# Feature attention in an eight-layer kernel: units pair by pair of feature groups, tile 0's maxima turned in two parts, the first pass four units ahead at first

## The chip, the cores and the metric

The kernel runs on one core of one Trainium2 chip. The metric is the device time of one execution, in microseconds (us), as the median of the runs. A core has TensorE (PE; its weight loads are listed as PEld), VectorE (DVE), ScalarE (ACT), GpSimd (POOL) and the queues that start DMAs (SP among them). TensorE's clock is granted in two levels, 0.50 of full speed (1.2 GHz) and 1.00 (2.4 GHz).

## The reference

Eight layers work one after the other on x, 1024 tokens of 256 features (16 sequences of 64), each adding to it. The layer of interest is the seventh, an attention between features, not tokens. Its query is the normalised x, key and value are both the context. Per sequence, the 64 tokens are cut into 8 heads of 8 tokens each:

```python
# q, k, v: (16, 64, 256) = (b, d, m or n); h = 8 heads, so d // h = c // h = 8
qh = q.reshape(b * h, d // h, m)
kh = k.reshape(b * h, d // h, -1)
vh = v.reshape(b * h, c // h, -1)
scale = 1.0 / jnp.sqrt(jnp.asarray(d // h, dtype=q.dtype))
qk = jnp.einsum('bdm,bdn->bmn', qh, kh) * scale      # 256 x 256 for each head
sm = jax.nn.softmax(qk, axis=-1)
ret = jnp.einsum('bmn,bcn->bcm', sm, vh)
```

## The kernel before

All eight layers are one program, with one queue of instructions for each engine and semaphores between them; the order in each queue is written out by hand. `feature_attention` follows a mixture of experts, whose last sums (`combine`) it runs itself through `x_of(t)` on VectorE, and is followed by `peer_mlp`, whose first work it starts at its end.

The 1024 tokens are 8 tiles of 128 (`NT`). A tile holds 16 heads of 8 tokens, that is 16 groups. In a strip of 32 partitions (`R`, four strips r = 0 to 3) there are four groups j = 0 to 3 (`J`), which come in two pairs `jp`. A tile is worked in `UNITS` = 4 units, one for each half of the 256 features (called b or nb) and pair `jp`; `halves(u)` says which unit does which. All matrices are float32, and each such matmul is two records in the trace.

A tile is passed twice.

First pass: `scores(u, r)` (line 2383) is one 32-row matmul for each strip r, four to a unit, one *step* each, `step = 4 * u + r`. It writes one bank of PSUM with 512 columns. `top(u, r)` (line 2238) on VectorE takes the negative maximum of each query's row into `nm`. When a tile's 16 maxima columns are made, `turn_maxima(t)` transposes them on TensorE (line 2417, two 128x128 transposes), ScalarE copies them (`maxima`, line 2312) and spreads them into `tm` (`placed(t, jp)`, line 2319, two copies for each pair), and GpSimd adds them to the masked queries `xm` (`less`, line 2183, once for each pair).

Second pass: `turned(u, pair)` (line 2408) computes the scores the other way round with the maximum already taken away, two strips for pair B (r = 2, 3) and two for pair A (r = 0, 1). `exps(u, ...)` (line 2329) on ScalarE takes the exponential of two banks at once, `values(u, j)` (line 2429) multiplies by the context into bank 7 (`VB`), eight 32-column matmuls a unit. At a tile's end `sums` (line 2336) copies that bank, `sort` (line 2447) picks sums and results apart by a table, `sorted_out` (line 2342) copies them and VectorE divides (line 2245 and on) and adds to `k.X`.

The first pass runs ahead of the second. Before the second begins, `FRONT` = 5 units of the first are issued; in unit 0 of the second loop it issues units 5 and 6, and from then on unit u + 6 (`AHEAD`). In the queue of TensorE, within unit u: two scores, turned(u, B), values(u-1, 0), turned(u, A), the other scores, values(u-1, 1). From unit `LAST` = 26 no scores are left.

Eight banks: the first 16 steps (`WIDE`) go round seven banks, 4, 5, 6, 0, 1, 2, 3. From then on scores have three banks, 4, 5 and 6 (`step_bank`), and the others belong to the second pass. A score waits until `top` has read what its bank held (`last_in_bank`). All on TensorE's queue behind a waiting score waits too.

GpSimd's queue at the start: zeroing `nm` (line 2198), `keys(0)`, two reciprocal roots for the normalisation (line 274), `queries(0)`, `keys(1)`, `queries(1)` (lines 2168 and 2175), memsets (2208, 2209), `values` copies of tiles 0 and 1 (2194), then `less(0)`. On VectorE, `norm(t)` (line 285) writes the normalised tile and `ln_stats_dve` (lines 266 to 268) makes its statistics; `x_of` is lines 1117 and 1118.

## Time and profile before

| | |
|---|---|
| median of 3 runs | 1093.72 us (1091.63 to 1097.1) |
| the profiled execution | 1091.79 us |
| its span (first to last instruction) | 1090.1 us |
| TensorE busy | 989.0 us, 91% |
| VectorE, ScalarE, GpSimd busy | 559.1, 361.1, 265.2 us |
| mean granted clock of TensorE | 0.947 |
| the feature attention's share | from 790.7 us to 948.3 us of the span |

Times in the rows are counted from the span's start. A matmul is listed from its start to its modelled end, so neighbouring ones overlap. A group in a timeline joins like instructions: its length is from the first start to the last end, and xN is their number.

### The profile page before, as it was taken

The page shows a single profiled execution, that of the slowest core. Times are in us where ns is not written, and L with a number is a line of the kernel's source. Part 1 is how long each engine was busy: PE and PEld are TensorE (multiplying, and loading weights), DVE is VectorE, ACT ScalarE, POOL GpSimd, SP SyncE. Part 2 cuts the span into 40 slices and gives each one's busy share as a digit, 9 for nine tenths or more (in the row PEclk, how much of TensorE's full clock was granted, in tenths as well). Part 3 has the DMA queues.
Part 4 walks back from the last instruction along what each step waited for, and adds up shares of the span by engine and source line. Part 5 has one row for each costly group of instructions (what it writes and reads, how often), then busy time and mean ns, then how long its engine had stood idle before and what let it go on. Part 6 is the DMA issues. An engine that isn't in the chain of part 4 may idle for free.

```text
span 1090.1 us, 18558 instructions
## 1 busy us (share of the span) xinstructions
PE 989.0 (91%) x7228; PEld 694.9 (64%) x7228; DVE 559.1 (51%) x1277; ACT 361.1 (33%) x687; POOL 265.2 (24%) x337
## 2 busy tenths in 40 slices
PE   5888999989999999968883999999689999997989
PEld 4665599546766667657663999999533343443467
DVE  7766523455435344465375121212277877666891
ACT  4662133242222121214210211111015666744750
POOL 6421342420000000022531122221252534202440
PEclk9996999999999999989985999999859999998989
DMA  9103033221001010054012866667214000010000
GB/s 281 46 2 107 11 97 93 83 59 31 25 29 40 26 40 11 6 154 145 1 64 83 299 213 227 222 217 271 64 34 154 10 2 1 15 64 1 0 11 29
DMA packets 39997, 88.96 MB, mean 82 GB/s; under 512 B 4712, under 2 KB 27592, under 8 KB 36584
## 3 DMA queue, kind: packets, MB, share of 16 engines
q1 hardware_dynamic: 32520, 73.60, 19.8%
q0 software_dynamic: 4080, 11.15, 3.6%
q10 hardware_dynamic: 3312, 3.02, 0.8%
q8 instruction: 60, 0.98, 0.4%
q14 instruction: 25, 0.20, 0.1%
HBM read 76.35 MB, written 11.40 MB: 81 GB/s over the span
## 4 chain that ended last, share of the span: by engine, by line
PE 75%; DVE 13%; ACT 5%; issue 3%; DMA 2%; POOL 2%; DVEq 0%; ACTq 0%; POOLq 0%
PE bank L358 21%; PE bank L1317 11%; PE bank L1336 7%; PE bank L1661 6%; PE bank L2383 5%; PE bank L2408 3%; PE bank L2429 3%; PE bank L2878 3%; PE bank L1307 3%; PE bank L1672 2%; PE bank L1637 2%; PE bank L2447 1%; PE bank L2884 1%; ACT big L587 1%; DVE big L2238 1%
## 5 line engine op out<-in xcount | busy, mean ns | idle before, releaser
L358 PE MATMUL bank<-XNT,big 128*128 128x512 f32 x296 | 136.8, 611 | 7.1 <-DVE big L2618 5.6
L1317 PE MATMUL bank<-big 128*128 128x128 f32 x1012 | 118.5, 277 | 0.1
L1317 PEld LDWEIGHTS bank<-big 128*128 128x128 f32 x1012 | 116.5, 194 | 0.5 <-issue 0.4
L274 POOL TENSOR_TENSOR rstd<-ve,half 128x1 f32<-128x1 f32 x48 | 27.8, 583 | 300.4 <-DVE ve L268 300.2
L2383 PE MATMUL bank<-big,xs 32*128 32x512 f32 x256 | 88.9, 732 | 12.1 <-DVE xs L285 10.4
L358 PEld LDWEIGHTS bank<-XNT,big 128*128 128x128 f32 x296 | 55.1, 193 | 69.7 <-issue 58.8
L2238 DVE TENSOR_REDUCE big<-bank 128x2 f32<-128x512 f32 x128 | 81.9, 685 | 20.3 <-PE bank L2383 19.6
L1095 DVE TENSOR_TENSOR big<-big,bank 128x640 f32<-128x640 f32 x23 | 18.9, 822 | 136.6 <-ACT big L1205 136.6
L1336 PE MATMUL bank<-big 128*128 (+1 forms) x368 | 87.2, 380 | 1.1 <-DVE big L1102 0.7
L2329 ACT ACTIVATE big<-bank 128x1024 f32<-128x1024 f32 x64 | 64.9, 1024 | 39.2 <-PE bank L2408 38.9
L1336 PEld LDWEIGHTS bank<-big 128*128 128x128 f32 (+1 forms) x368 | 66.3, 190 | 9.0 <-issue 1.9
L2408 PE MATMUL bank<-big 32*128 32x512 f32 x256 | 68.4, 659 | 1.6 <-POOL big L2183 1.4
L358 PE MATMUL bank<-CTXT,big 128*128 128x512 f32 (+1 forms) x192 | 66.9, 492 | 0.0
L1661 PE MATMUL bank<-big 128*128 128x256 f32 x256 | 63.7, 394 | 1.5 <-issue 1.2
L358 PE MATMUL bank<-big,CTXT 128*128 128x256 f32 (+1 forms) x224 | 57.9, 409 | 0.0
L1520 DVE COPY big<-bank 128x512 f32<-128x512 f32 x16 | 11.1, 692 | 88.7 <-PE bank L1646 88.7
L1661 PEld LDWEIGHTS bank<-big 128*128 128x128 f32 x256 | 47.1, 194 | 13.4 <-DVE X L1514 5.4
L1568 ACT COPY big<-bank 128x1024 f32<-128x1024 f32 x16 | 16.2, 1012 | 119.0 <-PE bank L1672 119.0
L977 POOL DMA_INDIRECT yg<-big x23 | 22.7, 986 | 135.3 <-DVE big L1102 127.9
L2383 PEld LDWEIGHTS bank<-big,xs 32*128 32x128 f32 x256 | 31.8, 207 | 35.1 <-issue 19.1
L358 PEld LDWEIGHTS bank<-big,CTXT 128*128 128x128 f32 x224 | 42.5, 190 | 17.3 <-issue 12.9
L358 PEld LDWEIGHTS bank<-CTXT,big 128*128 128x128 f32 x192 | 32.9, 196 | 30.2 <-issue 30.1
(356 smaller groups left out, 1753.0 us busy)
## 6 DMA issues: line engine op xcount, KB each, us to landing
big<-m_gu SPq DMA_DIRECT2D x23, 1408.0 KB, 6.0
big<-m_d SPq DMA_DIRECT2D x8, 768.0 KB
big<-a_qk SPq DMA_DIRECT2D x16, 256.0 KB, 2.9
yg<-big ACTq DMA_DIRECT2D x23, 128.0 KB, 2.0
big<-m_gu SPq DMA_DIRECT2D x8, 352.0 KB
big<-a_o SPq DMA_DIRECT2D x16, 128.0 KB, 2.0
xn<-XNT SPq DMA_DIRECT2D x8, 256.0 KB, 2.1
big<-f_keys SPq DMA_DIRECT2D x1, 2048.0 KB, 10.9
```

Source lines behind the costliest of these rows:

```text
L274: e.tensor_tensor(k.rstd[at % NT][:, :], k.ve[at % NT][:, :], k.half[:, 0:1], ALU.pow).then_inc(k.ln_rstd, 1)
L358: ins = e.matmul(out, a, b, start=start and n == 0, stop=stop and n == len(pairs) - 1)
L1307: ins = e.matmul(bank[:, GU[s % 2], c * F:(c + 1) * F], xgT[s % 2][:, kb, :], WB[:, bass.ds(at[s] + (kb * 2 * F + c * F), F)], start=kb == ...
L1317: ins = e.matmul(gu[:, n if n <= WHOLE else n + 1], gu_slot[s % SLOTS][:, c:c + P], xgT[s % 2][:, kb, :], start=kb == 0, stop=kb == KB - 1)
L1336: ins = e.matmul(bank[:, Y[s % 2], 0:D], hT[s % 2][0:row, b, :], WB[0:row, bass.ds(at[s] + (WGU + b * D), D) if LAG else bass.ds(at[s] * S ...
L1661: ins = e.matmul(bank[:, QK0 + j % 2, q * D:(q + 1) * D], cT[:, t * P:(t + 1) * P], wo[h % 2], start=True, stop=True)
L2238: e.tensor_reduce(nm[t % 2][:, b, c:c + 2 * G:G], k.bank[:, step_bank(step), :].rearrange("p (j n) -> p j n", j=2), AX.X, ALU.max, negate= ...
L2329: e.activation(pt[u % 2][:, r].rearrange("p r j n -> p r (j n)"), k.bank[:, b:b + 2, :], ACT.Exp, scale=float(G) ** -0.5).then_inc(S["ex"], 1)
L2383: e.matmul(bank[:, step_bank(step), :], k.xs[t % 2][q, b * P:(b + 1) * P], cm[t % 2][q, 2 * jp:2 * jp + 2].rearrange("p j n -> p (j n)"), ...
L2408: ins = e.matmul(bank[:, pair_banks(u, pair) + r % 2, :], cr[q, t, jp, nb * P:(nb + 1) * P], xm[t % 2][q, 2 * jp:2 * jp + 2].rearrange("p ...
L2429: ins = e.matmul(bank[r * R:(r + 1) * R, VB, jp * D:(jp + 1) * D], cv[t % 2][:, nb, r * J + 2 * jp + j], pt[u % 2][:, r, j], start=nb == 0 ...
L2878: e.matmul(bank[:, OUT + u % 2, 0:D], hT[:, u // UB, b, c], dn[:, b], start=b == 0, stop=False)
```

## The change

Four things are altered in `feature_attention`, all in the order of work; the matmuls, exponentials and sums stay the same in number and shape.

- `halves(u)` gives the units another order: both feature halves of the first pair, then both of the second. `turned` waits for the second pair's `less` at unit 2 of a tile, not at unit 1.
- The maxima of tile 0 are turned in two parts. The first pair's eight go to a new buffer `nm_first` and are transposed behind the scores of unit 2 (into bank 2), the whole tile's again for the second pair behind turned(0, A) (into bank 7). For tile 0, `maxima` and the transposes are therefore made twice, with two maxima sets; `placed(0, 1)` moves behind the exponentials of unit 0. `turns_made` counts the additional turn in all later waits. GpSimd zeroes one buffer more.
- The first 8 steps go round seven banks, not the first 16.
- Before the second pass, 4 units of scores are issued, not 5; then unit 4 in unit 0, units 5 and 6 in unit 1, 7 and 8 in unit 2, and u + 6 from unit 3 on. VectorE's `top`s follow. `norm(1)` comes after unit 1's maxima, not unit 0's; `x_of(3)` and those after it come one unit later.

```diff
@@ -2086,21 +2086,25 @@
     GT = P // G
     UNITS = 4
     NU = UNITS * NT
-    AHEAD, FRONT = UNITS + 2, UNITS + 1
+    AHEAD = UNITS + 2
     LAST = NU - AHEAD
     STEPS = 4
-    WIDE = STEPS * UNITS
+    WIDE = STEPS * 2
     TB, SBK, SBN, VB = 0, 4, 3, 7
     NTB, OB = TB + 2, TB + 3
     A_, B_ = 0, 1
     at0, done0 = 8 * l, LOADED + 8 * l
-    masks0 = k.count_masks(10)
+    masks0 = k.count_masks(11)
     A, B = Arena(k.big[:, 3384:16200], 16200 - 3384), Arena(k.late, 8800)
     cr, sel = A.take(NT, 2, D), A.take(4, P)
     tm = [A.take(J, D) for _ in (0, 1)]
     xm = [B.take(J, D) for _ in (0, 1)]
     cm = [B.take(J, D) for _ in (0, 1)]
     nm = [A.take(2, P) for _ in (0, 1)]
+    nm_first = A.take(2, P)
+
+    def maxima_of(t, jp):
+        return nm_first if t == 0 and jp == 0 else nm[t % 2]
     nT = [A.take(D) for _ in (0, 1)]
     cv = [A.take(KB, GT, R) for _ in (0, 1)]
     pt = [B.take(RG, 2, D) for _ in (0, 1)]
@@ -2124,7 +2128,7 @@
         e.wait_ge(S[name], start[name] + n)
 
     def halves(u):
-        return u // UNITS, u % UNITS // 2, u % 2
+        return u // UNITS, u % 2, u % UNITS // 2
 
     def step_bank(step):
 
@@ -2135,7 +2139,7 @@
 
     def units_ahead(u):
 
-        return [n for n in ((FRONT, AHEAD) if u == 0 else (u + AHEAD,)) if n < NU]
+        return [n for n in {0: (4,), 1: (5, 6), 2: (7, 8)}.get(u, (u + AHEAD,)) if n < NU]
 
     def pair_banks(u, pair):
 
@@ -2143,8 +2147,12 @@
             return TB + strips(pair)[0]
         return (4, 2, 0)[(2 * (u - LAST) + (pair == A_)) % 3]
 
-    def maxima_bank(t):
-        return spare_bank(UNITS * t - 2, NTB)
+    def maxima_bank(t, part=1):
+        return VB if t == 0 and part == 1 else spare_bank(UNITS * t - 2, NTB)
+
+    def turns_made(t):
+
+        return t + 2
 
     def result_bank(t):
         return spare_bank(UNITS * (t + 1) + 1, OB)
@@ -2194,8 +2202,8 @@
                     ins = e.tensor_copy(places(t % 2)[:, kb * G:(kb + 1) * G, j, 2 * G * j:2 * G * j + G], src[:, :, j])
             ins.then_inc(S["cv"], 1)
 
-        for p in (0, 1):
-            e.memset(nm[p], 0.0).then_inc(k.masks, 1)
+        for n in (nm_first, *nm):
+            e.memset(n, 0.0).then_inc(k.masks, 1)
         after(e, "ld", 16)
         keys(0)
         ln_rstd_pool(e, k, at0, 0)
@@ -2232,10 +2240,10 @@
             t, b, jp = halves(u)
             step = STEPS * u + r
             if t >= 2 and u % UNITS == 0 and r == 0:
-                after(e, "nt_ps", t - 1)
+                after(e, "nt_ps", turns_made(t - 2))
             after(e, "s_ps", step + 1)
             c = r * R + 2 * G * (1 - jp)
-            e.tensor_reduce(nm[t % 2][:, b, c:c + 2 * G:G],
+            e.tensor_reduce(maxima_of(t, jp)[:, b, c:c + 2 * G:G],
                             k.bank[:, step_bank(step), :].rearrange("p (j n) -> p j n", j=2), AX.X, ALU.max,
                             negate=True).then_inc(S["mx"], 1)
 
@@ -2254,8 +2262,8 @@
         def rest(u, half):
 
             t, n = divmod(u, UNITS)
-            if half == 1 and u < UNITS:
-                x_of(u + 4)
+            if half == 1 and u <= UNITS:
+                x_of(u + 3)
             if n == 0 and half == 0 and t + 2 < NT:
                 ln_stats_dve(e, k, ch, t + 2, t % 2)
             if n == 1 and half == 0 and t + 2 < NT:
@@ -2275,19 +2283,18 @@
                 k.front[6]["combine"](t)
                 e.wait_ge(k.x_tile, done0 - NT + t + 1)
 
-        e.wait_ge(k.masks, masks0 + 2)
+        e.wait_ge(k.masks, masks0 + 3)
         x_of(0)
         ln_stats_dve(e, k, ch, 0, 0)
         x_of(1)
         norm(0)
         ln_stats_dve(e, k, ch, 1, 1)
-        for u in range(FRONT):
+        for u in range(UNITS):
             for r in range(RG):
                 top(u, r)
-            if u == 0:
+            if u == 1:
                 norm(1)
         x_of(2)
-        x_of(3)
         for u in range(NU):
             ahead = [(n, r) for n in units_ahead(u) for r in range(RG)]
             for half in (0, 1):
@@ -2305,14 +2312,14 @@
     def act(e):
         e.sem_inc(k.xt_sb, NT)
 
-        def maxima(t):
-            after(e, "nt_ps", t + 1)
+        def maxima(t, part=1):
+            after(e, "nt_ps", turns_made(t) if part else 1)
             if t > 0:
                 after(e, "tm", 2 * t)
-            e.copy(nT[t % 2], k.bank[:, maxima_bank(t), 0:D]).then_inc(S["nm"], 1)
+            e.copy(nT[t % 2], k.bank[:, maxima_bank(t, part), 0:D]).then_inc(S["nm"], 1)
 
         def placed(t, jp):
-            after(e, "nm", t + 1)
+            after(e, "nm", turns_made(t) if t > 0 or jp else 1)
             if t >= 2:
                 after(e, "less", 2 * (t - 2) + jp + 1)
             for j in (2 * jp, 2 * jp + 1):
@@ -2341,16 +2348,19 @@
                 after(e, "v_sb", t)
             e.copy(od, k.bank[:, result_bank(t), :]).then_inc(S["od"], 1)
 
-        maxima(0)
+        maxima(0, 0)
         placed(0, 0)
-        placed(0, 1)
         for u in range(NU):
             t = u // UNITS
             more = t + 1 < NT
             exps(u, ((0, B_),))
+            if u == 0:
+                maxima(0)
             if u % UNITS == 2 and more:
                 maxima(t + 1)
             exps(u, ((1, A_),))
+            if u == 0:
+                placed(0, 1)
             if u % UNITS == 2 and more:
                 placed(t + 1, 0)
             if u % UNITS == 3 and more:
@@ -2388,11 +2398,11 @@
             t, nb, jp = halves(u)
             if u % UNITS == 0 and pair == B_:
                 after(e, "less", 2 * t + 1)
-            if u % UNITS == 1 and pair == B_:
+            if u % UNITS == 2 and pair == B_:
                 after(e, "less", 2 * t + 2)
             if u < LAST:
                 if u % UNITS == 3 and pair == B_ and t + 1 < NT:
-                    after(e, "nm", t + 2)
+                    after(e, "nm", turns_made(t + 1))
                 if u % UNITS == 2 and t > 0 and pair == B_:
                     after(e, "od", t)
                 if u > 0:
@@ -2409,12 +2419,12 @@
                                xm[t % 2][q, 2 * jp:2 * jp + 2].rearrange("p j n -> p (j n)"), start=True, stop=True)
             ins.then_inc(S["t_ps"], 1)
 
-        def turn_maxima(t):
-            after(e, "mx", STEPS * UNITS * (t + 1))
+        def turn_maxima(t, part=1):
+            after(e, "mx", STEPS * (UNITS * t + (UNITS if part else 2)))
             if 0 < t < NT - 1:
                 after(e, "ex", 2 * UNITS * t - 3)
             for b in (0, 1):
-                ins = e.transpose(bank[:, maxima_bank(t), b * P:(b + 1) * P], nm[t % 2][:, b, :], k.ident[:, :])
+                ins = e.transpose(bank[:, maxima_bank(t, part), b * P:(b + 1) * P], maxima_of(t, part)[:, b, :], k.ident[:, :])
             ins.then_inc(S["nt_ps"], 1)
 
         def values(u, j):
@@ -2441,7 +2451,7 @@
             elif t == NT - 1:
                 after(e, "od", t)
             else:
-                after(e, "nm", NT)
+                after(e, "nm", turns_made(NT - 1))
             for part in (0, 1):
                 for jp in (0, 1):
                     ins = e.matmul(bank[:, result_bank(t), part * D:(part + 1) * D], sel[:, 2 * part + jp],
@@ -2450,11 +2460,11 @@
 
         e.sem_inc(k.xt_ps, NT)
         after(e, "ld", 16)
-        for u in range(FRONT):
+        for u in range(UNITS):
             for r in range(RG):
                 scores(u, r)
-            if u == UNITS - 1:
-                turn_maxima(0)
+            if u == 2:
+                turn_maxima(0, 0)
         for u in range(NU):
             t = u // UNITS
             ahead = [(n, r) for n in units_ahead(u) for r in range(RG)]
@@ -2464,6 +2474,8 @@
             if 0 < u < LAST:
                 values(u - 1, 0)
             turned(u, A_)
+            if u == 0:
+                turn_maxima(0)
             for n, r in ahead[2 * (u > 0):]:
                 scores(n, r)
             if u % UNITS == 2 and t + 1 < NT:
```

## Rows read from the trace of the kernel before

**Rows 1.** The page: busy time, share of the span, instructions of each engine.
```profile
PE 989.0 (91%) x7228; PEld 694.9 (64%) x7228; DVE 559.1 (51%) x1277; ACT 361.1 (33%) x687; POOL 265.2 (24%) x337
```
**Rows 2.** Busy time of each engine by stretches; then granted clock, DMA share, GB/s.
```profile
790.67:794.00 3.33, 3.33 (x15) 1.75 (x16) 1.82 (x6) 0.00 (x0) 2.49 (x3) 0.50 0.27 82
794.00:797.60 3.60, 3.44 (x14) 1.46 (x10) 3.60 (x7) 0.00 (x0) 3.37 (x2) 0.97 0.01 2
797.60:801.10 3.50, 3.44 (x9) 1.49 (x6) 3.50 (x7) 0.00 (x0) 3.30 (x17) 0.50 0.00 0
...
806.60:812.30 5.70, 4.92 (x17) 1.88 (x17) 4.59 (x9) 2.55 (x3) 3.07 (x2) 0.50 0.13 27
812.30:818.00 5.70, 5.70 (x11) 2.97 (x12) 4.39 (x9) 0.08 (x1) 0.56 (x1) 0.50 0.21 65
818.00:821.40 3.40, 3.40 (x21) 1.08 (x18) 2.62 (x5) 0.99 (x1) 0.00 (x0) 0.51 0.00 0
...
827.58:924.00 96.42, 96.42 (x779) 38.10 (x779) 75.94 (x134) 62.91 (x86) 42.57 (x52) 1.00 0.12 47
924.00:948.30 24.30, 22.59 (x211) 11.30 (x208) 14.22 (x38) 18.36 (x29) 6.18 (x9) 1.00 0.01 1
```
**Rows 3.** The chain of waits: start us, us, what; unit 3 of the second loop.
```profile
827.58 0.63 PE bank L2383 x2
```
**Rows 4.** Timeline, first scores: start, us, engine, line, instructions joined.
```profile
790.67 2.09 PE L2383 MATMUL bank<-big,xs 32*128 32x512 f32 x8 [10.44 <-DVE xs L285]
...
792.51 2.88 PE L2383 MATMUL bank<-big,xs 32*128 32x512 f32 x11
...
792.75 2.48 DVE L2238 TENSOR_REDUCE big<-bank 128x2 f32<-128x512 f32 x4 [1.33 <-PE bank L2383]
...
795.84 7.26 DVE L2238 TENSOR_REDUCE big<-bank 128x2 f32<-128x512 f32 x12
796.00 1.89 POOL L2175 TENSOR_TENSOR big<-xs,strip 128x1024 f32<-128x1024 f32 x1 [0.23 <-DVE xs L285]
...
799.43 1.46 POOL L2194 COPY big<-CTXT 128x64 f32<-128x64 f32 x8
```
**Rows 5.** Timeline, from the turn of tile 0's maxima to the second pass.
```profile
803.15 0.69 PE L2417 MATMUL bank<-ident,big 128*128 128x128 f32 x2 [2.12 <-DVE big L2238]
...
803.77 2.08 PE L2383 MATMUL bank<-big,xs 32*128 32x512 f32 x6
803.88 0.37 ACT L2312 COPY big<-bank 128x256 f32<-128x256 f32 x1 [28.79 <-PE bank L2417]
804.28 1.70 ACT L2319 ACTIVATE big<-big,strip 128x256 f32<-128x256 f32 x4
805.33 2.49 POOL L2183 TENSOR_TENSOR big<-big 128x512 f32<-128x512 f32 x2 [4.44 <-ACT big L2319]
...
806.65 1.24 PE L2408 MATMUL bank<-big 32*128 32x512 f32 x3
...
810.44 1.94 ACT L2329 ACTIVATE big<-bank 128x1024 f32<-128x1024 f32 x2 [3.15 <-PE bank L2408]
```
**Rows 6.** ScalarE's exponentials by line: duration ns min/median/max, first and last start.
```profile
L2329 ACT ACT_TABLE_LOAD  x1: 1283/1283/1283, 806.0 to 806.0; - x1
```
**Rows 7.** Timeline, unit 1 of the second pass, with the clock back.
```profile
820.31 1.08 PE L2429 MATMUL bank<-big 128*32 128x256 f32 x8
...
821.33 0.70 PE L2383 MATMUL bank<-big,xs 32*128 32x512 f32 x2
...
821.86 0.59 PE L2383 MATMUL bank<-big,xs 32*128 32x512 f32 x2
```
**Rows 8.** Timeline near the stage's end, unit 29.
```profile
933.58 1.28 POOL L2183 TENSOR_TENSOR big<-big 128x512 f32<-128x512 f32 x1 [1.28 <-ACT big L2319]
934.91 1.14 PE L2408 MATMUL bank<-big 32*128 32x512 f32 x8 [0.41 <-POOL big L2183]
935.35 0.59 ACT L2336 COPY big<-bank 128x512 f32<-128x512 f32 x1
```

## Prediction

> **What bounds the kernel now.** I read the page first. TensorE is busy for 91% of the span and the other engines for far less [rows 1], so the question is where TensorE works without a wait and where it doesn't. The clock line of the page is near full almost everywhere, but a slice of it is 27 us long, so I then cut the feature attention into stretches [rows 2]. It runs from 790.67, its first score matmul, to 948.3. Three stretches differ.
>
> From 827.58 to 924 TensorE is busy all the time at a granted clock of 1.00, 96.42 of 96.42 us, with VectorE at 75.94 and ScalarE at 62.91. No wait ends late here; TensorE's own instructions set the length. Reordering the four units of a tile doesn't change their number or shape, so this stretch keeps its length.
>
> From 790.67 to 827.58, which is in the chain of waits the start of unit 3 in the second loop [rows 3], 36.91 us pass. TensorE's granted clock is 0.50 (1.2 GHz) up to 794, 0.97 (all but 2.4 GHz) to 797.6, and 0.50 again until 821.4. This is the first pass, which fills the pipeline, and it is where the change works. It is bound by turns: VectorE needs 0.605 us for each maximum (12 in 7.26 us) [rows 4], and once the first seven banks are used TensorE may write a bank only after the maximum of its last content. After 806.6 three banks rotate. In the stretch 812.3 to 818, TensorE is shown busy throughout, but only 11 records fall in it; it writes one score at a time, in turn with VectorE [rows 2].
>
> From 924 to 948.3 the stage runs dry: 22.59 of 24.30 us busy. One wait there belongs to the change, at 934.91 [rows 8].
>
> **The prices.** At the low clock a score needs 2.08 us from its start until VectorE can read it, whether one, three or four of different row strips run together: three take 2.08, four 2.09 [rows 4, 5]. The next matmul on the same strip starts 1.84 us after it (790.67, then 792.51). At the high clock the same two records take 0.70 and 0.59 and overlap to 1.12 us [rows 7]. I add 0.05 us for each semaphore, from the gap between the end of the transposes, 803.84, and the copy at 803.88 [rows 5]. A bank comes round at the low clock in 0.69 + 0.05 + 2.08 + 0.05 = 2.87 us, for three banks 0.96 us a step. At the high clock that is 1.91, or 0.64 a step. VectorE alone would want 0.605. So a step that rides in a group of four is cheap, and a step that has its bank alone is dear at the low clock.
>
> **The change, part by part.**
>
> *Seven banks for 8 steps, not for 16 (WIDE).* Steps 0 to 7 are as before; the maximum of step 7 ends at 792.75 + 7 x 0.605 + 0.69 = 797.67, since norm(1) no longer stands between. Steps 7 and 8 both fall on bank 4. Step 7 may start at 793.5, when the maximum of step 0 is made, and is through by 795.6 even at the low clock. From there to 797.7 TensorE stands still, where before it kept on, and VectorE waits for step 8 until 799.8. Steps 8, 9 and 10 run together; step 11 follows the maximum of 8 at 800.55.
>
> *Turning the maxima in two parts.* turn_maxima(0, 0) stands behind step 11. Step 11's second half streams until about 802.4, so the two transposes run 802.5 to 803.2, against 803.15 before, and all that follows keeps its length: from the transposes' start to the end of less(0, 0) before it was 806.60 minus 803.15, 3.45 us; two of four placed copies on ScalarE stand ahead of it either way [rows 5]. So less(0, 0) ends at 805.95 and turned(0) starts at 806.03, against 806.65. The half-set of maxima comes 8 steps earlier, but the starvation of banks eats nearly all of it: the gain is 0.6 us. GpSimd isn't in the way. queries(1) follows norm(1) at 798.1 and takes 1.89, the memsets 1.54, the copies 1.46 [rows 4]; it is free at 803.0, and needed at 804.7. The added memset costs at most what the eight of its kind take together, 1.54 us (from 797.89, where queries(1) ends, to 799.43) [rows 4]; it lies ahead of the stage's first score, which waits for TensorE's operands from VectorE, not GpSimd (its releaser is line 285), so I count nothing; uncovered it would be those 1.54 us at most.
>
> *One step fewer ahead (four units, not five; then 4, 5 and 6, 7 and 8).* Steps 12 and 13 start 0.62 after the transposes, at 803.12; 14 behind the maximum of 11 (802.66 + 0.69 + 0.05), at 803.41; 15 behind that of 12 (805.23 + 0.74), at 805.97. Step 15 shares strip 3 with turned(0, B), as step 19 did before, when exps(0, B) came 3.8 us after that score (806.63, 810.44): now at 809.7. turn_maxima(0) then needs the last maximum (808.8) and the strips: 809.6 to 810.3. Scores 16 to 18 start 0.62 after it, at 810.2; 19 behind the maximum of 16 (+ 2.08 + 0.79), at 813.1; 20 0.6 later; 21, whose bank waits for the maximum of 18 behind tile 2's statistics (0.85 us), with turned(1, B) at 815.15. values(0, 0) follows 1.84 + 0.1 later and takes the 1.0 us at the low clock from 820.31 to 821.32 [rows 7]: 817.1 to 818.1, and turned(1, A) with scores 22 and 23 starts at 818.1, against 821.32 [rows 7]. Here the new order is 3.2 us ahead, but has issued 8 score steps fewer. These 8 are not gone: they stand in units 1 and 2, four more in each, one at a time through three banks, at 0.64 (high clock) or 0.96 us (low) a step. So 8 steps cost 5.1 to 7.7 us, less 3.2 is +1.9 to +4.5, and the bubbles where a group of four interrupts the rotation come on top.
>
> *x_of one tile later.* Before, both x_of(2) and x_of(3) stood between the maxima of steps 19 and 20. In the new order x_of(2) lies in a rest of VectorE. x_of(3) now holds the maximum of step 20 back, from 815.8 to 816.85; the next score that needs it is step 23 at 818.1, so it costs nothing.
>
> *Order of units (halves), and the wait on less.* Before, unit 29 needed the second half of less(7), which ended at 934.86; TensorE idled 0.41 us for it [rows 8]. It now needs it at unit 30. What is late next is ScalarE: its copy of the sums can't start before 935.35, and exps(29, B) stands behind it. That gives about 0.1 us, not 0.4. If TensorE were free earlier, the same copy would still hold values(28).
>
> *Identity copies between the exponentials.* The trace shows one table load of 1283 ns in the whole stage, though seven tiles have such copies between their exponentials [rows 6]. Moving placed(0, 1) there costs no second load; if it did, 2.6 us of ScalarE would lie in its rests of several us.
>
> *The skill against the trace.* Between 128-row transposes and 32-row scores the trace shows 0.62 us from the first transpose to the next score (803.15, 803.77), with no visible stop. The Trainium skill, TensorEngine Tiling (Array Packing), Key Properties, says that a change of the tiling mode drains TensorE; that speaks against a second turn in the first pass. By the rows the second turn costs 0.6 us, already counted; by the rule it also waits until all four strips have run out, at most one 2.08 us score more, and the sum would be 1099.3 (rival F). No row here shows such a price.
>
> **The sum, and the three clocks.** Continuing step by step from 818.1:
> - High clock from 818.1 on: step 24 at 819.1, 25 at 819.95, 27 at 821.6; unit 2 starts at 823.25, step 35 at 828.0, the turn at 829.1, unit 3 at 830.04. Against 827.58: +2.5.
> - High for unit 1's scores, lost by 821.4 in their single steps, regained in unit 2: unit 2 starts at 824.45, steps 33 to 35 at 830.05, 830.65, 831.05, unit 3 at 833.1: +5.5.
> - Low until the end of unit 2: steps 24 to 27 at 819.95, 820.95, 821.55, 822.8, unit 2 at 825.75, step 35 at 833.25, unit 3 at 836.8: +9.2.
>
> What speaks for the middle: before, the clock rose after the dense group of the first scores and again after 818 to 821.4, when scores, turned and values filled all strips; it fell at 797.6 after a stretch of single steps, and stayed at 0.50 through 806.6 to 818 [rows 2]. The new order has its dense stretch from 815.15 to 819.1, then single steps again. So it should rise once and be lost once. Sum: 1091.79 (the profiled execution, its span 1090.1 and 1.7 around it) + 5.5 - 0.1 = 1097.2. The median of the three runs, 1093.72, lies 1.9 above the profiled one; both bases are in the range.
>
> **Rivals.**
> - *A (33%)*, the middle case: 1097.2; its own range 1095 to 1099.
> - *B (28%)*, the clock stays high once gained: 1091.79 + 2.4 = 1094.2. For it: 818.1 is followed by 1 us of four strips, more than after 794. Against: the row of 794 to 797.6 shows TensorE nearly all busy and the clock still fell.
> - *C (15%)*, slower: the clock isn't regained before unit 3: 1091.79 + 9.1 = 1100.9. It decides where the stretch 815.15 to 819.1 doesn't bring it up; 806.6 to 812.3 was much work and didn't.
> - *D (14%)*, faster: the clock stays high through steps 8 to 15. Then less(0, 0) is bound by GpSimd, free at 803.0, turned(0) starts at 804.35, and turned(1, A) at about 811.7, 6.4 before case B; unit 3 is at 823.6, so -4.0 and 1087.7. It decides at 797.7: against it, TensorE has had 2 us of rest there.
> - *E (5%)*, what I can't see, such as a wait in the steady part: no row shows one. Either sign, 1080 to 1110.
> - *F (5%)*, the second turn stops the matmuls until all four strips are empty: one score's 2.08 us on top of A, 1099.3. It decides if the transposes start later than the last strip's stream ends.
>
> **How the numbers follow.** About 0.5%, 5.5 us, is what a measurement of this kernel can tell from no change. A straddles it at +5.4: half of its 33%, C less 0.01, F and part of E give 0.16 + 0.14 + 0.05: 0.35 slower. Faster by over 5.5 needs more than D: a part of D and E, 0.07. The rest, 0.58, is within. The range leaves out the lower half of D and the upper end of C taken from the median: 1090.0 to 1101.5.
>
> **What the profile after would show.** Maxima of steps 0 to 7 without a gap, then a rest of VectorE of about 1.8 us before the ninth; the first transposes at about 11.8 us after the first score, turned(0) at 15.4 (16.0 before), turned(1, A) at 27.4 (30.65 before), and unit 3's start at 42.4 (36.9 before), the stretch from there to the last scores as long as before (96.4 us); one table load. TensorE's wait for less(7) near the end gone. I am wrong if the clock in the first 40 us is high where I put it low, if step 8 doesn't wait for step 7's maximum, or if TensorE waits in the steady part.

## The result, and the profile after

| | before | changed |
|---|---|---|
| median of the runs | 1093.3 us (12 runs) | 1101.43 us (1097.43 to 1103.17, 12 runs) |
| ratio to before | | 1.0067, 95% interval 1.0051 to 1.0083 |
| profiled execution; its span | 1091.79; 1090.1 us | 1102.17; 1100.4 us |

The change makes the kernel 8.1 us slower. Two profiles of a kernel of this length differ by some us in other layers; here the first score comes 4.67 us later already (795.34, before 790.67), which the change can't cause: narrow_only below, which alters nothing ahead of the first score, has it at 795.47. So I measure the stage by itself: from its first score to the start of the last result matmuls. That was 155.59 us before (790.67 to 946.26) and is 163.60 now (795.34 to 958.94): 8.0 us longer, about the difference of the medians.

The page of the changed kernel: span, then busy time, share and instructions of each engine [rows 1 before].

```profile
span 1100.4 us, 18560 instructions
...
PE 996.3 (91%) x7230; PEld 696.0 (63%) x7230; DVE 559.3 (51%) x1277; ACT 361.4 (33%) x688; POOL 266.4 (24%) x338
```

The stretches of the changed kernel (PE, PEld, DVE, ACT, POOL busy, granted clock, DMA share, GB/s), against [rows 2]:

```profile
795.34:798.67 3.33, 3.33 (x15) 1.74 (x16) 1.82 (x6) 0.00 (x0) 2.50 (x3) 0.51 0.30 82
798.67:802.27 3.60, 0.81 (x5) 0.00 (x0) 3.60 (x8) 0.00 (x0) 1.76 (x1) 0.96 0.01 2
802.27:805.90 3.63, 2.78 (x7) 1.00 (x8) 1.79 (x5) 0.00 (x0) 3.20 (x8) 0.50 0.00 0
...
822.70:830.50 7.80, 7.80 (x28) 2.87 (x24) 4.70 (x9) 1.49 (x2) 0.00 (x0) 0.50 0.11 33
830.50:838.35 7.85, 7.85 (x47) 2.83 (x43) 5.95 (x11) 1.49 (x3) 0.00 (x0) 0.86 0.00 0
838.35:851.26 12.91, 11.70 (x92) 3.90 (x88) 11.76 (x21) 9.03 (x12) 8.05 (x9) 1.00 0.05 16
851.26:936.70 85.44, 85.44 (x692) 34.08 (x691) 66.80 (x117) 54.01 (x75) 34.97 (x43) 1.00 0.13 50
```

The second row is the rest of TensorE ahead of step 8: 0.81 us busy of 3.60, against 3.44 of 3.60 before. The clock is then 0.50 for long: cut finer, it is still 0.50 from 828.34 to 831.84 and 0.87 from 831.84 to 835.34, so it came back some 37 us after the first score, 2 us into unit 2; before it was back after 31. And the row 838.35 to 851.26 is not like before: TensorE is busy for 11.70 of 12.91 us in what was the steady part.

VectorE in the first pass, timeline of the changed kernel [rows 4 before]:

```profile
797.42 4.88 DVE L2246 TENSOR_REDUCE big<-bank 128x2 f32<-128x512 f32 x8 [1.33 <-PE bank L2393]
...
804.46 1.89 DVE L2246 TENSOR_REDUCE big<-bank 128x2 f32<-128x512 f32 x3 [1.84 <-PE bank L2393]
807.31 0.69 DVE L2246 TENSOR_REDUCE big<-bank 128x2 f32<-128x512 f32 x1 [0.97 <-PE bank L2393]
809.93 1.89 DVE L2246 TENSOR_REDUCE big<-bank 128x2 f32<-128x512 f32 x3 [1.93 <-PE bank L2393]
812.79 0.69 DVE L2246 TENSOR_REDUCE big<-bank 128x2 f32<-128x512 f32 x1 [0.97 <-PE bank L2393]
```

Eight maxima in 4.88 us without a gap, then eight with four waits for TensorE, 5.71 us in all. The 16th ends at 813.48, 18.1 us after the first score; before it was 12.4. TensorE's side of it:

```profile
802.35 2.08 PE L2393 MATMUL bank<-big,xs 32*128 32x512 f32 x6 [2.87 <-DVE big L2246]
805.21 2.07 PE L2393 MATMUL bank<-big,xs 32*128 32x512 f32 x2 [0.77 <-DVE big L2246]
807.21 0.69 PE L2427 MATMUL bank<-ident,big 128*128 128x128 f32 x2
...
810.70 1.23 PE L2418 MATMUL bank<-big 32*128 32x512 f32 x3
...
814.39 0.69 PE L2427 MATMUL bank<-ident,big 128*128 128x128 f32 x2
```

turned(0) starts at 810.70, 15.4 us after the first score (before 16.0), turned(1, A) at 823.0, 27.7 (before 30.65). In the chain of waits, from which [rows 3] has 827.58, unit 2 starts at 830.64, 35.3 after the first score, and unit 3 at 838.41, 43.1 (before 36.9). From there to the first result matmuls it is 12.9 us, before 10.7. This is what stands in those 12.9 us:

```profile
846.69 0.51 DVE L1117 SCALAR_TENSOR_TENSOR X<-XNT,big,X 128x256 f32<-128x256 f32 x1
...
847.24 2.19 DVE L1118 SCALAR_TENSOR_TENSOR X<-XNT,big,X 128x256 f32<-128x256 f32 x1
847.26 1.89 POOL L2176 TENSOR_TENSOR big<-big,strip 128x1024 f32<-128x1024 f32 x1
...
850.21 0.69 PE L2393 MATMUL bank<-big,xs 32*128 32x512 f32 x1 [1.21 <-DVE big L2246]
```

The second operation of x_of(7), which takes 0.48 us for each other tile, takes 2.19. It starts with GpSimd's keys(3) and ends 0.3 us after it, and TensorE waits 1.21 us for the maximum behind it.

So the 8.0 us are +6.2 up to unit 3, +2.2 from there to the first result matmuls, and -0.4 behind.

### The profile page after: what moved, and what is told of

Same layout as the page of the kernel before. It is cut to its first block, busy times and chain, and to the rows that moved or that the text cites. A ratio compares the mean times of both kernels' runs of the same rounds, so it can differ in the third digit from the quotient of the medians.

```text
span 1100.4 us, 18560 instructions
## 1 busy us (share of the span) xinstructions
PE 996.3 (91%) x7230; PEld 696.0 (63%) x7230; DVE 559.3 (51%) x1277; ACT 361.4 (33%) x688; POOL 266.4 (24%) x338
## 3 DMA queue, kind: packets, MB, share of 16 engines
q10 hardware_dynamic: 3312, 3.02, 0.8%
## 4 chain that ended last, share of the span: by engine, by line
PE 75%; DVE 13%; ACT 5%; issue 3%; DMA 2%; POOL 2%; DVEq 0%; ACTq 0%; POOLq 0%
PE bank L358 21%; PE bank L1317 10%; PE bank L1336 7%; PE bank L1661 5%; PE bank L2393 5%; PE bank L2418 3%; PE bank L2439 3%; PE bank L2890 3%; PE bank L1307 2%; PE bank L1672 2%; PE bank L1637 2%; PE bank L2457 1%; PE bank L2896 1%; DVE big L2246 1%; DMA big<-yg,big 1%
## 5 line engine op out<-in xcount | busy, mean ns | idle before, releaser
L2393 PE MATMUL bank<-big,xs 32*128 32x512 f32 x256 | 92.4, 748 | 16.8 <-DVE xs L285 10.5
L2246 DVE TENSOR_REDUCE big<-bank 128x2 f32<-128x512 f32 x128 | 82.3, 686 | 28.0 <-PE bank L2393 27.4
L1661 PEld LDWEIGHTS bank<-big 128*128 128x128 f32 x256 | 47.0, 194 | 13.5 <-DVE X L1514 5.8
L358 PEld LDWEIGHTS bank<-big,CTXT 128*128 128x128 f32 x224 | 42.5, 190 | 17.3 <-issue 12.9
## 6 DMA issues: line engine op xcount, KB each, us to landing
big<-f_keys SPq DMA_DIRECT2D x1, 2048.0 KB, 10.7
```

Source lines behind the costliest of these rows:

```text
L358: ins = e.matmul(out, a, b, start=start and n == 0, stop=stop and n == len(pairs) - 1)
L1661: ins = e.matmul(bank[:, QK0 + j % 2, q * D:(q + 1) * D], cT[:, t * P:(t + 1) * P], wo[h % 2], start=True, stop=True)
L2246: e.tensor_reduce(maxima_of(t, jp)[:, b, c:c + 2 * G:G], k.bank[:, step_bank(step), :].rearrange("p (j n) -> p j n", j=2), AX.X, ALU.max, ...
L2393: e.matmul(bank[:, step_bank(step), :], k.xs[t % 2][q, b * P:(b + 1) * P], cm[t % 2][q, 2 * jp:2 * jp + 2].rearrange("p j n -> p (j n)"), ...
```

## The experiments

Each ran beside the kernel before. The ratios are known to some 0.2%, 2 us, so for smaller things I use the stage's length in the profile. It is one execution each. Where the clock is the same it repeats closely: successive results stood 17.10 or 17.11 us apart through the steady part of every kernel that had the new order, but for one tile of clock_fill. The clock is not the same in all of them, though, and a stage length contains what the clock did in that one execution. The last column therefore says when, in the first 60 us after the first score, the granted clock stood at 1.00 (read to 0.5 us; 0.50 otherwise).

| kernel | first score | last results | stage, us | ratio to before (95%) | clock at 1.00, us after the first score |
|---|---|---|---|---|---|
| before | 790.67 | 946.26 | 155.6 | | 3.5 to 7, from 31 on |
| changed | 795.34 | 958.94 | 163.6 | 1.0067 (1.0051 to 1.0083) | 3.5 to 6.5, from 37.5 on |
| narrow_only | 795.47 | 954.45 | 159.0 | 1.0036 (1.0013 to 1.0058) | 3.5 to 7, 24 to 27.5, from 34 on |
| wide_16 | 790.19 | 950.26 | 160.1 | 1.0062 (1.0036 to 1.0088) | 3.5 to 7, 17.5 to 20.5, from 34.5 on |
| x_early | 790.52 | 950.83 | 160.3 | 1.0042 (1.0017 to 1.0066) | 30 to 33.5, from 36.5 on |
| x_late | 789.34 | 946.76 | 157.4 | 1.0000 (0.9982 to 1.0018) | 3.5 to 7, from 31 on |
| root_first | 790.18 | 952.12 | 161.9 | 1.0054 (1.0032 to 1.0076) | 3.5 to 7, from 37.5 on |
| order_only | 795.47 | 950.58 | 155.1 | 0.9993 (0.9974 to 1.0012) | 3.5 to 7, from 31 on |
| both | 795.14 | 952.88 | 157.7 | 1.0007 (0.9986 to 1.0027) | 3 to 6.5, from 34 on |
| five_ahead | 791.07 | 946.36 | 155.3 | 0.9998 (0.9980 to 1.0016) | 3.5 to 7, from 31 on |
| sooner | 792.81 | 950.52 | 157.7 | 1.0018 (1.0001 to 1.0036) | 3 to 6.5, 30.5 to 34, from 37.5 on |
| four_one_turn | 795.95 | 957.17 | 161.2 | 1.0039 (1.0016 to 1.0062) | 3.5 to 6.5, 27 to 30.5, 37.5 to 41, from 44.5 on |
| early_turn | 794.37 | 952.33 | 158.0 | 1.0002 (0.9981 to 1.0023) | 3.5 to 6.5, 24 to 27, 34 to 37.5, from 41 on |
| clock_fill | 792.72 | 955.28 | 162.6 | 1.0040 (1.0018 to 1.0062) | 3.5 to 20.5, 34 to 51, from 58 on |

### The rotation of banks: narrow_only, wide_16

The kernel before, with one edit:

```diff
-    WIDE = STEPS * UNITS
+    WIDE = STEPS * 2
```

> The kernel before with only 8 steps round seven banks, all else as before. Theory 1: steps 8 to 15 then go through three banks one by one at the low clock, the 16th maximum comes 4 to 5 us later, and all behind it: ratio 1.004. Theory 2: the first pass is bound by what comes behind it, and the rest of VectorE is made up for in unit 0: under 1.5 us, ratio 1.000 to 1.0015.

3.4 us by the stage, 1.0036. The timeline of VectorE in narrow_only shows the same waits as the changed kernel:

```profile
805.26 1.89 DVE L2238 TENSOR_REDUCE big<-bank 128x2 f32<-128x512 f32 x3 [2.16 <-PE bank L2383]
808.12 1.89 DVE L2238 TENSOR_REDUCE big<-bank 128x2 f32<-128x512 f32 x3 [0.97 <-PE bank L2383]
810.97 1.29 DVE L2238 TENSOR_REDUCE big<-bank 128x2 f32<-128x512 f32 x2 [0.96 <-PE bank L2383]
```

The first turn's transposes come 16.85 us after the first score and not 12.48, 4.4 us later. Theory 1 holds: about 1 us of this is made up for behind it, in an execution whose clock rose once more between 24 and 27.5 us, and the rest is not. The changed kernel with this part put back:

```diff
-    WIDE = STEPS * 2
+    WIDE = STEPS * UNITS
-        return VB if t == 0 and part == 1 else spare_bank(UNITS * t - 2, NTB)
+        return VB if t == 0 else spare_bank(UNITS * t - 2, NTB)
...
+            if u == 0 and pair == B_:
+                after(e, "mx", STEPS * UNITS - 2)
```

> The changed kernel with the first 16 steps round seven banks; both turns of tile 0's maxima go to bank 7, and turned(0, B) waits for the first 14 maxima. Theory 1: the starvation of banks is the largest cost. VectorE no longer rests before step 8; second pass begins at 13.6 us after the first score (15.4 in the changed kernel), turned(1, A) at 24.1 (27.7), and the kernel is 3.5 us faster than the changed one, 4.6 over before, ratio 1.004. Theory 2: the low clock and the single steps of units 1 and 2 cost it all the same; then it gains under 1 us, ratio 1.0065 to 1.0075.

The stage is 3.5 us shorter, as expected, and the milestones came as expected too: turned(0) 13.5 us after the first score, turned(1, A) 23.7. The ratio's own interval is too wide to tell 1.0062 from 1.0067 or 1.004. VectorE's sixteen maxima have only norm(1) between them (timelines of wide_16; its first score is at 790.19):

```profile
792.27 4.88 DVE L2246 TENSOR_REDUCE big<-bank 128x2 f32<-128x512 f32 x8 [1.33 <-PE bank L2393]
...
797.38 5.03 DVE L2246 TENSOR_REDUCE big<-bank 128x2 f32<-128x512 f32 x8
802.33 1.62 DVE L1117 SCALAR_TENSOR_TENSOR X<-XNT,big,X 128x256 f32<-128x256 f32 x1
...
802.41 1.26 POOL L2191 TENSOR_TENSOR big<-big 128x512 f32<-128x512 f32 x1
...
803.72 2.09 PE L2420 MATMUL bank<-big 32*128 32x512 f32 x8 [3.53 <-POOL big L2191]
```

### x_of one unit later: x_early, x_late, root_first

The changed kernel with x_of where it was:

```diff
-            if half == 1 and u <= UNITS:
-                x_of(u + 3)
+            if half == 1 and u < UNITS:
+                x_of(u + 4)
...
         x_of(2)
+        x_of(3)
         for u in range(NU):
```

> The changed kernel with one thing put back: x_of(2) and x_of(3) stand ahead of the second loop again and x_of(u+4) in unit u. Theory 1: of the 8.1 us lost, 2.2 came after unit 3 of the second loop, because x_of(7) fell together with GpSimd's keys(3) and its second operation took 2.19 us in place of 0.48. Then x_of(7) takes 0.48 again, the steady part has no waits of TensorE for VectorE, and the kernel is 2 us faster than the changed one: 6 us over before, ratio 1.0055. Theory 2: VectorE simply has too little lead after the first pass, wherever x_of stands; then the waits stay and the time is that of the changed kernel, ratio 1.007 to 1.0075.

The stage is 3.3 us shorter, and line 1118 takes 0.48 us for all tiles. From the start of unit 3 to the first results there is no wait for VectorE, and this part takes 10.6 us, 2.3 less than in the changed kernel. That is what the theory names. The other 0.9 us lie ahead of unit 3: in this run the clock also rose earlier (0.74 in its stretch 817 to 824, where the changed kernel has 0.50 at the same distance), and what is x_of's part of them stays open. The same move the other way, in the kernel before:

> The kernel before with x_of(3) to x_of(7) one unit later, alone. Theory 1: what hurts is that the second operation of x_of(7) meets GpSimd's keys(3), which runs from 836.2 to 838.1 there; x_of(7) now comes in unit 4's second half, at about 836.7 to 838: it takes up to 2.2 us in place of 0.48, and some of it reaches TensorE. Stage 155.6 plus 0.5 to 1.9, less the 1.1 us for which x_of(3) held back the maximum of step 20: 155.0 to 156.5, ratio 0.9995 to 1.001. Theory 2: with the full lead of maxima that this kernel has in unit 4, nothing reaches TensorE even if it is stretched: 154.5 to 155.

1.8 us longer by the stage, none by the ratio, whose interval reaches to 1.0018. By the chain of waits it is 0.4 us less up to unit 3 and 2.2 more from there to the first results. The timelines of VectorE and GpSimd in x_late show the collision once more:

```profile
834.67 2.19 DVE L1118 SCALAR_TENSOR_TENSOR X<-XNT,big,X 128x256 f32<-128x256 f32 x1
836.90 1.29 DVE L2238 TENSOR_REDUCE big<-bank 128x2 f32<-128x512 f32 x2
```
```profile
834.70 1.89 POOL L2168 TENSOR_TENSOR big<-big,strip 128x1024 f32<-128x1024 f32 x1
```

So the lead that the kernel before has doesn't cover it; theory 2 is out. What remains to show is that it is the GpSimd operation. In the changed kernel I swapped two operations in GpSimd's queue and left x_of where it is:

```diff
         for t in range(2, NT):
-            keys(t)
             ln_rstd_pool(e, k, at0 + t, t % 2)
+            keys(t)
```

> The changed kernel; in GpSimd's queue each later tile's reciprocal root (0.55 us) stands ahead of keys, not behind it. x_of stays one unit late. In the changed kernel x_of(7)'s second operation started at 847.24 and keys(3) at 847.26, and both ran to about 849.4. Theory 1: what stretches the VectorE operation is GpSimd's keys(3) at the same moment; with the root at that moment the operation takes 0.48 us, or is stretched by the root's 0.55 at most, and the stage is 1.5 to 2.3 us shorter than 163.6: 161.3 to 162.1, ratio 1.005. Theory 2: the operation is slow for another reason (the copy of the other tiles' data, a DMA's write to the same buffer): it takes 2.19 again and the stage 163.6.

Timelines of VectorE and GpSimd in root_first:

```profile
842.16 0.48 DVE L1118 SCALAR_TENSOR_TENSOR X<-XNT,big,X 128x256 f32<-128x256 f32 x1
...
843.88 0.85 DVE L285 TENSOR_SCALAR xs<-X,mv,rstd 128x256 f32<-128x256 f32 x1
```
```profile
842.18 0.55 POOL L274 TENSOR_TENSOR rstd<-ve,half 128x1 f32<-128x1 f32 x1
842.70 1.89 POOL L2176 TENSOR_TENSOR big<-big,strip 128x1024 f32<-128x1024 f32 x1
```

0.48 us again with x_of still late, and the stage 1.7 us shorter than the changed kernel's. The clock was the same in both runs, so this comparison is a clean one. That is the collision, shown from both sides. keys(3) now meets norm(3) (line 285), which takes 0.85 in place of 0.41; so not all of the 2.2 comes back.

The time from unit 3 to the first results says it for all kernels: 12.9 us where x_of(7) meets keys(3) (the changed kernel, wide_16, x_late), 11.2 in root_first, 10.6 or 10.7 in before, order_only, narrow_only, five_ahead, both, sooner and x_early. The other three had a low clock within it or, in clock_fill, the collision again.

The Trainium skill says of this, in SBUF — State Buffer, Who interferes with whom, that a VectorE instruction with two inputs in SBUF contends with a GpSimd instruction that reads SBUF, and calls the contention an exclusive lock. The trace agrees that they contend: the operation was 1.71 us longer beside a GpSimd operation of 1.89. Whether it stood still or ran slower, one length doesn't show. Maxima, whose input is in PSUM, stand at 0.67 to 0.70 us beside GpSimd's work everywhere.

### The order of units: order_only

```diff
-        return u // UNITS, u % UNITS // 2, u % 2
+        return u // UNITS, u % 2, u % UNITS // 2
...
-            if u % UNITS == 1 and pair == B_:
+            if u % UNITS == 2 and pair == B_:
```

> The kernel before with the new order of units (and the wait on less at unit 2 of a tile) alone. Theory 1: nothing but the wait at 934.91 goes, behind which ScalarE's copy is next: 0.1 us faster, ratio 1.000. In the changed kernel the result matmuls stood 17.11 us apart, not 17.21; if that comes from the order, it is 0.8 us faster in all, ratio 0.9993. Theory 2: the order hurts somewhere in the steady part: over 1.002.

0.5 us shorter by the stage, and within the noise by the ratio. Of the 0.5, four periods give 0.1 each: in the chain of waits of order_only the results stand at

```profile
843.00 1.92 PE bank L2447 x8
860.10 1.92 PE bank L2447 x8
877.21 1.92 PE bank L2447 x8
```

17.1 us apart, before 17.2. TensorE's waits near the stage's end (who is waited for: us in total, times, longest) in the kernel before, and then in order_only:

```profile
PE bank L2408 <- POOL big L2183: 1.4, 2, 0.9
PE bank L2408 <- ACT big L2342: 0.2, 1, 0.2
```
```profile
PE bank L2408 <- POOL big L2183: 0.9, 1, 0.9
PE bank L2429 <- ACT big L2336: 0.4, 1, 0.4
PE bank L2408 <- ACT big L2342: 0.2, 1, 0.2
```

The second wait for less is gone, and 0.4 us for ScalarE's copy of the sums (line 2336) stands in its place.

### What is left: both, five_ahead, sooner, four_one_turn

both is the changed kernel with the edits of wide_16 and x_early together.

> The two mends together: seven banks for 16 steps, and x_of where it was. What is left of the change is the order of units, the turn in two parts and four units ahead at first. By its profile the stage, from the first score to the start of the last result matmuls, took 155.6 us before, 163.6 in the changed kernel, 160.3 with x_of put back and 160.1 with the wide rotation. Theory 1: the two costs lie one behind the other and add: 156.8, ratio 1.001. Theory 2: they overlap (both come from VectorE's maxima being late), and what is left, single steps in units 1 and 2, costs 2 us or more of its own: 158 to 159.5, ratio 1.002 to 1.0035.

157.7 lies between the two, nearer to theory 2. To say which part of the change keeps 2.6 us over order_only, I changed only how far ahead the first pass is.

```diff
 # five_ahead, from both; FRONT is 5 again
-        return [n for n in {0: (4,), 1: (5, 6), 2: (7, 8)}.get(u, (u + AHEAD,)) if n < NU]
+        return [n for n in {0: (5, 6)}.get(u, (u + AHEAD,)) if n < NU]
 # sooner, from both
+        return [n for n in {0: (4, 5), 1: (6, 7), 2: (8,)}.get(u, (u + AHEAD,)) if n < NU]
```

> As both, but five units are scored ahead of the second loop and units 5 and 6 in its unit 0, as in the kernel before. What is left of the change is the order of units and the turn in two parts. The stage took 155.1 us with the order alone and 157.8 in both. Theory 1: what both still loses is that fewer scores are ahead: VectorE rests in units 0 and 1, and the maxima it then owes stand one by one in TensorE's queue. With five ahead the stage is 154.4 to 155.3, ratio 0.998 to 0.9995. Theory 2: the additional turn and the copies behind the exponentials cost; then it stays over 156.5.

155.3: theory 1. With the clock as in order_only, the turn in two parts neither gains nor loses: 155.3 against 155.1. Of both's 157.7, the 2.4 us more all lie ahead of unit 3, which starts 39.6 us after the first score and not 37.1; the clock came back 3 us later there, and how much of the 2.4 is the clock isn't separated. Timeline of VectorE, the first maximum behind the sixteenth, in five_ahead, then in sooner:

```profile
804.91 1.89 DVE L2246 TENSOR_REDUCE big<-bank 128x2 f32<-128x512 f32 x3 [1.63 <-PE bank L2394]
```
```profile
811.15 1.89 DVE L2246 TENSOR_REDUCE big<-bank 128x2 f32<-128x512 f32 x3 [3.03 <-PE bank L2394]
```

> As both, still four units ahead of the second loop, but units 4 and 5 are scored in its unit 0, 6 and 7 in unit 1, 8 in unit 2 (both: 4; 5, 6; 7, 8). Theory 1 (VectorE's rests in units 0 and 1 are the loss): a unit's maxima move one unit earlier, the stage is 0.5 to 1.5 us shorter than both's 157.8, ratio 1.000. Theory 2: the number of single steps in the queue is what costs; it is the same here, and so is the time within 0.3 us.

157.7, as both: theory 1 as I put it there falls. Moving scores from units 1 and 2 to units 0 and 1 brings nothing. The rest of 3.03 us ahead of unit 4's first maximum stays as it is (3.02 in both), because unit 4's scores still stand behind turned(0) and the second turn; it is this start of unit 4 that five_ahead moves.

four_one_turn is order_only with `FRONT = UNITS` and the amounts ahead of the changed kernel.

> The kernel before with the new order of units and the new amounts ahead (four units, then 4; 5, 6; 7, 8), but one turn of tile 0's maxima and seven banks for 16 steps. Theory 1: turned(0) starts where it did, at 15.9 us after the first score (15.3 at the best, since unit 4's scores no longer stand ahead of it: the turn at 12.5 plus 3.4), the second pass is not earlier than with two turns, and the stage is that of both or up to 2.5 us longer: 157.8 to 160.3, ratio 1.002 to 1.004. Theory 2: the two turns cost more than they bring; the stage is shorter than 157.5.

161.2, longer than theory 1 allowed. Behind the sixteenth maximum VectorE has two x_of to do and then waits 5.50 us:

```profile
815.83 1.29 DVE L2238 TENSOR_REDUCE big<-bank 128x2 f32<-128x512 f32 x2 [5.50 <-PE bank L2383]
```

So with four units ahead the turn in two parts is worth up to 3.5 us, and with five ahead nothing. Not all of the 3.5 is the wait. Up to the turn of tile 1's maxima four_one_turn is 1.9 us behind both (40.5 and 38.6 us after the first score). The other 1.6 comes from there to the first results, with the same instructions and a clock of 0.50 for 3.5 us, where both had 1.00. Whether the low clock there belongs to the order or to this one execution, which was 5.4 us longer than the kernel's median, isn't shown.

### The start of the second pass, and the clock: early_turn, clock_fill

early_turn is both, with norm(1) behind unit 0's maxima and this in GpSimd's queue:

```diff
         queries(1)
+        less(0, (0,))
...
         values(1)
-        less(0)
+        less(0, (1,))
```

> As both, and GpSimd's queue and VectorE's are put in the order that the first turn wants: norm(1) behind unit 0's maxima as in the kernel before, and the first half of less(0) ahead of the memsets and the copies for values, the second half behind them. Theory 1: in the wide rotation GpSimd holds the second pass (turned(0) at 13.5 us after the first score, 1.2 us behind its copies); now it starts at 11.3, the second turn and unit 4's scores follow about 2.5 us earlier, and the stage is 2.5 us shorter than in both: 154.3 if that is 156.8, ratio 0.999. Theory 2: the start of the second pass doesn't matter, since VectorE's maxima set the pace: the same as both within 0.7 us.

turned(0) starts 11.9 us after the first score and not 13.5, and the stage is 0.2 us longer, which is theory 2's number.

```profile
806.23 2.09 PE L2422 MATMUL bank<-big 32*128 32x512 f32 x8 [1.45 <-DVE big L2247]
```

It also shows that I had named the wrong wait: in this kernel the bank's maximum (line 2247) is what turned(0) waits for last, not GpSimd.

Theory 2's reason isn't shown, though. At the turn of tile 1's maxima early_turn is 1.3 us ahead of both (37.3 and 38.6 us after the first score). From there to the first results it takes 13.05 us and both 11.53, with the same instructions. The clock differs, here from 36.5 to 40 us after the first score, in early_turn and then in both:

```profile
830.87:834.37 3.50, 3.50 (x21) 0.92 (x18) 2.40 (x5) 2.09 (x4) 0.00 (x0) 0.63 0.00 0
```
```profile
831.64:835.14 3.50, 3.50 (x20) 1.35 (x23) 3.45 (x7) 0.98 (x2) 0.00 (x0) 1.00 0.00 0
```

So an earlier second pass did bring 1.3 us in this execution, and 1.5 went where the clock was low. Why the clock fell again isn't settled, nor whether it does so in every execution of early_turn.

clock_fill is the changed kernel with

```diff
+        def filler(n):
+            for _ in range(n):
+                e.matmul(bank[:, VB, :], k.ident[:, :], k.CTXT[:, 0, 0:512], start=True, stop=True)
...
                 scores(u, r)
+                filler({7: 3, 10: 1, 11: 1, 14: 1}.get(STEPS * u + r, 0))
```

> The changed kernel with six matmuls more on TensorE, 128 rows by 512 columns, in its rests of the first pass: three behind step 7, one behind each of steps 10, 11 and 14. They write bank 7, which nobody reads before it is written again, and change no result. Theory 1: the low clock (0.50 from 7 us after the first score to 37 us) is a large part of the cost; the clock stays high through steps 8 to 15, the 16th maximum ends at about 15.5 us and not 18.1, and the stage is 2 to 3 us shorter than the changed kernel's 163.6. Theory 2: the waits are for VectorE and banks, the matmuls added stand in the way of the next score, and the stage gains nothing or loses up to 1.5 us.

The stretches of clock_fill:

```profile
799.70:811.70 12.00, 11.13 (x44) 3.87 (x44) 8.09 (x15) 5.56 (x9) 6.47 (x19) 1.00 0.07 23
811.70:815.20 3.50, 3.17 (x19) 0.59 (x17) 3.43 (x6) 0.95 (x1) 3.50 (x3) 0.71 0.00 0
815.20:825.70 10.50, 10.50 (x40) 3.95 (x40) 7.31 (x14) 1.72 (x3) 0.00 (x0) 0.50 0.07 25
...
844.85:864.70 19.85, 19.85 (x139) 8.12 (x138) 12.66 (x22) 9.97 (x14) 6.91 (x9) 0.85 0.48 201
```

The clock is 1.00 through steps 8 to 15, and the 16th maximum ends 15.4 us after the first score, as theory 1 says (18.1 without). The first result matmuls come 3.8 us earlier than in the changed kernel. Then 2.8 of it is given back: in 844.85 to 864.70 the clock is 0.85, and that tile takes 19.87 us, not 17.11. So the price of the low clock is shown, 2.7 us on these eight steps, and as a whole only 1.0 us stays. Why the clock fell in a stretch where TensorE is shown busy throughout isn't settled. It is the only fall behind the first results, but early_turn and four_one_turn also have 3.5 us of 0.50 in the 6 us from 36 and from 39 us after the first score, with TensorE busy for 6.00 of 6.00.

## Why the prediction came out as it did

The sign was right, and so was the mechanism up to unit 3; behind it a cost is missing. The forecast was 1097.2 and the measured median 1101.43, between case C's 1100.9 and the range's end at 1101.5, so that it lies in the range by luck. The 4.2 us between forecast and median are 1.5 from the base (1091.79 against the median 1093.3), 0.7 from the stretch up to unit 3, 2.2 from the collision that the prediction didn't have, and -0.3 from the order of units. The change itself was taken as +5.4 and measured as +8.1. By steps:

- **Seven banks for 8 steps: right, to 0.1 us.** The maximum of step 7 ended 6.96 us after the first score (7.0 forecast), step 8 waited for it, step 11 came at 805.21, that is 9.87 (9.88), the transposes at 11.87 (11.8), turned(0) at 15.36 (15.36). Alone it costs 3.4 us, and 3.5 in the changed kernel.
- **The gain of the two turns: right in the first pass**, 0.6 us for turned(0). Rival F falls: the transposes at 814.39 stand 0.99 us behind the last strip's start, the usual distance of two records at the low clock.
- **One step fewer ahead: right in kind.** turned(1, A) came 27.7 us after the first score (27.4). both less five_ahead gives the price, 2.4 us, with the 3 us more of low clock in it.
- **The clock: another course than forecast, and nearly the same sum.** I took it as risen once behind 818.1, that is 27.4 us after the first score, and lost again (+5.5, case A), and gave a clock that stays low until unit 3 only 15% (case C). It stayed at 0.50 up to unit 2, which started 35.3 us after the first score, as in case C (35.1; A has 33.8). Then it rose within unit 2, which took 7.8 us (A: 8.65, C: 11.05): +6.2 up to unit 3. The +9.2 of case C needed a clock low to unit 3's start. So A's number was nearly met, but by a course that no case had: C's up to unit 2 and a rise within it. That is luck.
- **The step that failed: x_of one tile later.** The prediction said that it "costs nothing". I had looked only for which maxima it holds up in the first pass, and not for what stands on GpSimd at its new place. x_of(7) met keys(3): +2.2, of which 1.7 came back when the two were put apart; when only x_of was moved in the kernel before, the same stretch grew by 2.2 too, and the stage by 1.8. A wait of TensorE in the steady part was among the signs named for being wrong, and in rival E with 5%: by this sign the prediction was wrong here.
- **Order of units: right that what is late next is ScalarE's copy**; the 0.1 us forecast there didn't come at all. The statement that the steady stretch keeps its length was wrong by -0.1 us a tile.
- **x_of(2) in a rest, norm(1) later, the added memset, the table load**: nothing of these shows in the time. x_of(2) stays at 0.47 and 0.48 us in the changed kernel; in wide_16, both and sooner its first operation meets the first half of less(0) and takes 1.62, ahead of a rest of VectorE of over 3 us.

Put on one behind the other, from 155.6: order and two turns together -0.3 (five_ahead), four ahead +2.4 (both), x_of later +2.3 (wide_16), the short rotation +3.5 (the changed kernel, 163.6). Such a row of kernels adds up whatever the parts are. That they are near what each costs alone is shown for the rotation (3.4) and for x_of (1.8), not for four ahead. No kernel here beats the one before by more than the measurement tells; order_only is the best by the stage, 0.5 us.

## What to carry to other kernels

Starting the second stage of a pipeline earlier brought nothing by the end here: with five units ahead the two turns gained nothing, and 1.3 us won at the start of the second pass were gone again after a stretch of low clock. The rests that the engine between the stages (here VectorE) got in the fill were mostly paid later: of the 4.4 us in narrow_only, 3.4 reached the end. Buffers taken from the fill phase to start something else early are dear, more so if the producer runs at a low clock meanwhile. Before two stage lengths from single profiles are compared, their granted clocks must be. And an operation that is moved on one engine must be checked against what the other engines do at its new place, not only against its own queue: 0.48 us became 2.19 by standing beside one GpSimd operation.

## What the runs showed of the hardware that was not expected

- A VectorE operation on two SBUF inputs beside GpSimd's 128x1024 multiplication took 2.19 us in place of 0.48, in the changed kernel and in x_late alike, and 0.48 beside GpSimd's 128x1 power (root_first). norm, a VectorE operation with one tensor input, went from 0.41 to 0.85 beside the same multiplication, and to 1.46 for the four tiles after it in root_first, without a cost to the stage that shows.
- The start may decide who is stretched. In the changed kernel line 1118 for x_of(6) started at 842.92, 0.13 us ahead of a GpSimd addition of 128x512 (843.05): it took 0.49, and the addition 1.49 in place of 1.27. In wide_16 line 1117 started 0.08 us ahead of one: it took 1.62, and the addition its usual 1.26. These are readings of two starts, not an experiment.
- Six additional matmuls in TensorE's rests held the clock at 1.00 for 12 us, and a score was then ready after 1.12 us, not 2.08 (801.85 and 806.29 in clock_fill):

```profile
801.85 1.12 PE L2393 MATMUL bank<-big,xs 32*128 32x512 f32 x2
...
806.29 1.12 PE L2393 MATMUL bank<-big,xs 32*128 32x512 f32 x2
```

- Two matmul orders with the same instructions differ by 0.1 us a tile (17.21 and 17.11); the cause is open.
